# A transformer layer on one core: requests to a two-bank PSUM ring spaced out, and large transfers issued behind the attention loads

## What is computed

```python
# phase 1: conditioned RMS norm, 16 heads of 32, q and k normalised per head
xn = rms_norm(x, g_norm) * (1 + scale) + shift          # scale, shift from cond
q, k, v = heads(xn @ W_qkv); q = rms_norm(q, g_q); k = rms_norm(k, g_k)
o = softmax(q @ k.T * 32 ** -0.5) @ v
x1 = o + o @ W_out
# phase 2: latent attention, rotary parts, causal
kv_d, q_d = n1 @ kv_d_w, n1 @ q_d_w                     # n1 = rmsnorm(x1, ln1_w)
k = concat(kv_d @ k_u_w, rope(n1 @ rope_k_w)); q = concat(q_d @ q_u_w, rope(q_d @ rope_q_w))
h = x1 + softmax(causal(q @ k.T * scale)) @ (kv_d @ v_u_w) @ o_w
# then: shared expert + the two best of seven routed experts, on n2 = rmsnorm(h, ln2_w)
out = x + h + moe(n2)
```

## Time and profile before

| what | value |
|---|---|
| median of three runs | 1292.82 us (1291.26 to 1294.52) |
| the profiled execution, its time | 1290.86 us |
| its span in the trace | 1289.1 us |
| busy: PE, DVE, ACT, POOL | 91%, 58%, 44%, 23% of the span |
| mean granted PE clock | 0.970 of 2.4 GHz |
| transfers | 178.42 MB, 138 GB/s on the mean |

### The profile page before, as it was taken

The page is one execution under the profiler, slowest core; times in us unless marked ns, Lnnn a source line. Parts: engine busy times, 40 slices in busy tenths (PEclk is TensorE's granted clock), DMA queues, the critical chain, the costliest instruction groups (busy, mean ns, idle before and its releaser), DMA issues.

```text
span 1289.1 us, 18670 instructions
## 1 busy us (share of the span) xinstructions
PE 1169.7 (91%) x6059; PEld 825.7 (64%) x6059; DVE 744.4 (58%) x1807; ACT 572.3 (44%) x1248; POOL 290.7 (23%) x244
## 2 busy tenths in 40 slices
PE   5979999999999889999999989989999999999970
PEld 5745555665566446557767757766657888888850
DVE  6565675477545856666565575566364774444433
ACT  3324464345443555455465454455264753222210
POOL 1313122100210031001011200200124464555530
PEclk9979999999999999999999999999899999999995
DMA  7064243125311732352284264265357744555559
GB/s 255 33 180 131 65 136 112 50 86 184 99 50 58 225 107 57 99 189 88 88 259 149 86 234 122 84 201 176 86 186 232 262 152 105 109 108 113 115 134 331
DMA packets 88127, 178.42 MB, mean 138 GB/s; under 512 B 12609, under 2 KB 23265, under 8 KB 86497
## 3 DMA queue, kind: packets, MB, share of 16 engines
q1 hardware_dynamic: 79216, 156.90, 37.4%
q0 software_dynamic: 8512, 19.93, 8.2%
q10 hardware_dynamic: 304, 0.40, 0.2%
HBM read 110.86 MB, written 65.27 MB: 137 GB/s over the span
## 4 chain that ended last, share of the span: by engine, by line
PE 77%; DVE 8%; DMA 5%; ACT 4%; issue 3%; SPq 1%; POOL 0%; DVEq 0%; ACTq 0%; POOLq 0%
PE psum L862 14%; PE psum L681 9%; PE psum L682 8%; PE psum L683 8%; PE psum L846 6%; PE psum L825 6%; PE psum L690 4%; PE psum L940 4%; PE psum L942 4%; PE psum L941 4%; PE psum L967 2%; PE psum L969 2%; PE psum L968 2%; PE psum L909 2%; PE psum L772 2%
## 5 line engine op out<-in xcount | busy, mean ns | idle before, releaser
L1174 ACT ACTIVATE probs<-psum 128x512 f32<-128x512 f32 (+3 forms) x512 | 257.3, 517 | 231.5 <-PE psum L849 120.6
L825 PE MATMUL psum<-stack 96*128 96x512 f32 (+3 forms) x512 | 210.2, 416 | 8.6 <-DMA stack<-split_s 4.0
L1583 DVE TENSOR_REDUCE nmax<-psum 128x1 f32<-128x512 f32 x256 | 170.5, 684 | 77.0 <-PE psum L825 73.2
L846 PE MATMUL psum<-stack 97*128 97x512 f32 (+3 forms) x512 | 197.3, 386 | 16.8 <-ACT probs L1174 15.4
L862 PE MATMUL psum<-probs,vals 128*33 128x512 f32 (+3 forms) x1024 | 209.4, 531 | 0.0
L1586 DVE CUSTOM_DVE_ANT_0 psum<-psum,causal 128x128 f32<-128x128 f32 (+3 forms) x256 | 123.0, 501 | 21.0 <-PE psum L825 19.4
L825 PEld LDWEIGHTS psum<-stack 96*128 96x128 f32 x512 | 100.0, 196 | 46.3 <-issue 23.7
L846 PEld LDWEIGHTS psum<-stack 97*128 97x128 f32 x512 | 99.0, 193 | 40.0 <-ACT probs L1174 25.8
L862 PEld LDWEIGHTS psum<-probs,vals 128*33 128x33 f32 x1024 | 49.8, 112 | 99.6 <-issue 65.5
L681 PE MATMUL psum<-w_hi,xh 128*128 128x512 f32 (+1 forms) x256 | 95.4, 373 | 4.2 <-DVEq L1449 2.5
L682 PE MATMUL psum<-w_hi,xl 128*128 128x512 f32 (+1 forms) x256 | 93.6, 366 | 0.0
(11 more groups left out here) (238 smaller groups left out, 2338.0 us busy)
## 6 DMA issues: line engine op xcount, KB each, us to landing
stack<-split_s SPq DMA_DIRECT2D x378, 128.0 KB, 3.0
split_s<-split SPq DMA_DIRECT2D x64, 512.0 KB, 3.0
xt<-in_x_dram SPq DMA_DIRECT2D x4, 1024.0 KB, 5.2
x_s<-yt SPq DMA_DIRECT2D x4, 1024.0 KB, 5.0
xt<-x_s SPq DMA_DIRECT2D x4, 1024.0 KB, 4.8
yt<-in_x_dram SPq DMA_DIRECT2D x4, 1024.0 KB, 5.6
res<-x_s SPq DMA_DIRECT2D x4, 1024.0 KB, 8.2
acc_s<-yt SPq DMA_DIRECT2D x4, 1024.0 KB, 6.0
```

The source lines that it names most:

```text
L825: sq.filled(nc.tensor.matmul(psum[:, sq.bank(M), 0:n], st[:, 0, t * P:(t + 1) * P], st[:, 1, 0:n], start=True, stop=True), M)
L846: last = nc.tensor.matmul(psum[:, bank, lo:S], st[:, 1, t * P:(t + 1) * P], st[:, 0, lo:S], start=True, stop=not masked)
L1174: sk.cleared(nc.scalar.activation(probs[:, M % NX, lo:S], psum[:, sk.bank(M), lo:S], ACT.Exp, scale=SCALE), M)
L1583: sq.cleared(V.tensor_reduce(out, psum[:, sq.bank(M), :], AX.X, ALU.max, negate=True), M)
```

## The change

Nothing is computed differently, and no instruction comes or goes apart from a few that wait. Numbers in the table of steps change, one line moves the last `x` key of a sequence from step 63 to step 0 of the next block, and SP's large transfers move by three steps, which puts each behind the six loads of its neighbourhood. `w_raw` moves from step 46 to 41.

```diff
-        put((23, 27, 31, 35) if phase(j) == 1 else (25, 29, 33, 37), each("out", i, NT))
+        put((23, 28, 31, 36) if phase(j) == 1 else (25, 29, 33, 39), each("out", i, NT))
         if phase(i) == 2:
-            put((28, 33, 36, 41), each("square2", i, NT))
-            put((43, 43, 44, 44), each("norm2", i, 4))
-            put((47, 47, 49, 49), each("scale2", i, NT))
-            put((51, 52, 54, 55), each("x2", i, NC))
-            put((59, 62), each("router", i, 2))
+            put((28, 33, 36, 42), each("square2", i, NT))
+            put((44, 44, 45, 45), each("norm2", i, 4))
+            put((46, 46, 47, 47), each("scale2", i, NT))
+            put((49, 52, 54, 55), each("x2", i, NC))
+            put((60, 62), each("router", i, 2))
+    if k and j < NB:
+        put((0,), [("x", j, NC - 1)])
...
-        put((26, 30, 33, 39) if k == B - 2 else (39, 47, 55, 59), each("v", j, NT))
+        put((25, 30, 33, 39) if k == B - 2 else (39, 47, 54, 55), each("v", j, NT))
...
-        put((27, 31, 35, 39), each("v", j, NT))
+        put((27, 31, 36, 41), each("v", j, NT))
...
-        put((60, 61, 62, 63), each("x", after, NC))
+        put((60, 62, 63), each("x", after, NC - 1))
...
-                    if i >= B and m == 14:
+                    if i >= B and m == 17:
                         load_residuals(i)
-                    if m == (22 if k == 0 else 6) and k + 2 < NB:
+                    if m == (25 if k == 0 else 9) and k + 2 < NB:
                         load_x(k + 2)
-                    if i >= 0 and phase(i) == 1 and m == 46:
+                    if i >= 0 and phase(i) == 1 and m == 49:
                         store_x1(i)
...
-                    if k == B - 2 and m == 46:
+                    if k == B - 2 and m == 41:
                         ring.wait_full(sp, ("v", B - 1, NT - 1))
...
-                    if k == B and m == 54:
+                    if k == B and m == 57:
                         ring.wait_full(sp, ("out", B - 1, NT - 1))
```

More of the change, by code:

```diff
@@ L579, in _ @@
                             load_pair(k + next_, q)
-                    if i >= B and m == 14:
+                    if i >= B and m == 17:
                         load_residuals(i)
-                    if m == (22 if k == 0 else 6) and k + 2 < NB:
+                    if m == (25 if k == 0 else 9) and k + 2 < NB:
                         load_x(k + 2)
-                    if i >= 0 and phase(i) == 1 and m == 46:
+                    if i >= 0 and phase(i) == 1 and m == 49:
                         store_x1(i)
-                    if i >= 0 and phase(i) == 2 and m == 46:
+                    if i >= 0 and phase(i) == 2 and m == 49:
                         store_acc(i)
-                    if i >= 0 and phase(i) == 2 and m == 54:
+                    if i >= 0 and phase(i) == 2 and m == 57:
                         store_x2(i)
-                    if k == B - 2 and m == 46:
+                    if k == B - 2 and m == 41:
                         ring.wait_full(sp, ("v", B - 1, NT - 1))
@@ L602, in _ @@
                         sp.dma_start(ln2row[:, :], ln2_d.rearrange("(a n) -> a n", a=1).broadcast_to([P, D])).then_inc(o2_ld, 16)
-                    if k == NB - 1 and m == 38:
+                    if k == NB - 1 and m == 41:
                         ring.wait_full(sp, ("v", LAST, NT - 1))
```

## The result

The changed kernel is slower, by 0.7%: 1301.56 us in the median of 20 runs (1294.73 to 1306.52) against 1292.75 us of the kernel before, measured beside it in as many. The ratio is 1.0072, with a 95% interval of 1.0055 to 1.0089, or +9.3 us (7.1 to 11.5). The forecast was 1283.6 us with 1275 to 1293 as its range, so the time lies outside it, on the wrong side.

What follows compares the result with a forecast made beforehand. The PE was taken to set the pace, with some 53 us of holes in the blocks. The terms summed to -9.2 us on the profiled 1290.86, so 1281.7; the median lying 2.0 us higher gave 1283.6, range 1275 to 1293.

Steps and rivals of the forecast that it cites:

- Block 7's residuals: Block 7, step 24: residuals now directly ahead of `max_rows` land about 908.2, `scores_t` waits for them: +0.7 us.
- The low clock stays: Block 7, step 24: the half-speed clock from 906.90 for 6.8 us, behind a 2.27 us hole, remains after the change.
- block 7 would then gain: Rival, chance 0.15: small transfers pass large ones, `wo_raw` is in time, block 7 gains 2.5 us; 1276 us.
- Second norm and router: Blocks 5 and 6: `x2` 0 starts earlier, -2.6 us; block 7: 0; `router` 0 one step later: -1.0 us.
- the second rival: The DVE is the bound that holes hide; 10.3 us of gains come to nothing, 1293.9 us; chance 0.20.
- The circle: Blocks 3 to 6: `turn` 1 k waits through `out` 3, `o_hi`, `o_lo`, +3.4 us; `v` 2 one step later, -2.8.
- The early blocks: `v` 3 earlier -1.6, `out` 3 spaced -1.1, block ends (0 to 3, 5) -2.5, exponential at block start -1.4 us.
- The weights: Block 2: `w_raw` at step 41 removes waits for `max_rows`, -4.6 us; block 4: `wo_raw` and `ln_row` late, +4.3 us.
- the signs: What would show it, among others: block 4 has a hole of 4 to 5 us and a low clock behind it.
- 0.10 for slower: Chance of a slower kernel: backlog behind `out` 3 and `turn_o` 0 costs up to 4.1 us a block, 1296.6 us.
- three terms with a plus: Waits newly made: `turn` 1 k in blocks 3 to 6 +3.4, `ln_row` in block 4 +4.3, `max_rows` in block 7 +0.7 us.

Runs made afterwards that it cites:

- e4: The kernel before with only the load of the residuals moved, from step 14 to 17, behind the stack's loads: 1298.14 us, ratio 1.0048.
- e3: The changed kernel with only the load of the residuals back at step 14: 1294.84 us, ratio 1.0015 to the kernel before.
- e1: The kernel before with all the change's moves of transfers in SP's queue, and the old table of steps: 1297.21 us, ratio 1.0039.
- e5: The kernel before with only `w_raw` moved, from step 46 to 41 of block 2: 1288.35 us, ratio 0.9973.
- e8: The changed kernel with all transfers at their old steps and `out` 3, `v` 2 and `v` 3 of blocks 3 to 6 as before: 1291.13 us, ratio 0.9989.
- e2: The changed kernel with all transfers back at their old steps, so the new table of steps alone: 1294.36 us, ratio 1.0012 to the kernel before.
- e7: The kernel before with the new table's early part; `out`, `v`, second norm, `x2` and router of blocks 3 to 7 as before: 1287.53 us, ratio 0.9969.
- e9: The kernel before with only `wo_raw` and `ln_row` of block 4 moved, from step 54 to 57: 1298.51 us, ratio 1.0043.
- e10: The kernel of e8 with block 7's second norm and router also as before: 1287.84 us, ratio 0.9970 to the kernel before.
- e11: The kernel of e7 with `w_raw` also moved to step 41: 1287.59 us, ratio 0.9966 to the kernel before.
- e6: The kernel before with only block 7's residuals moved, to step 20, one step behind `max_rows`: 1292.24 us, ratio 0.9994.
- e12: The kernel of e11 with block 7's residuals also moved to step 20, one step behind `max_rows`: 1283.33 us, ratio 0.9935 to the kernel before.

## Why the prediction failed

**Block 7's residuals: the step that failed most.** The prediction took the mechanism from `max_rows`'s 6.48 us, and it holds: "if `max_rows` waits for it, `scores_t` of step 24 starts then". The term was mis-sized. It was worked out from one `res` that landed 8.0 us after issue, gave 908.2, and so +0.7 us. Measured are +6.2 us alone (e4) and +7.4 in the changed kernel (e3). Two things were wrong in it.

First, the landing. The last part of `max_rows` came 11.0 us after the issue of `res` in e4, 8.9 in e1 and 12.9 in the changed kernel, not 8.0. The 8.0 us were taken from block 5, where a step is longer and the other transfers stand farther off. For block 7 itself the trace of before had a longer one (transfers issued in 894 to 895):

```profile
res<-x_s SPq DMA_DIRECT2D x1, 1024.0 KB, 10.2
```

Reckoned with 10.2, `max_rows` would have landed at about 910.4; in e4 it was 910.7. Loads that are issued while `res` is under way do not make a long one by themselves: the row of 8.0 us had them too, 4.1 us behind its issue. Over all traces of blocks 5 to 7, `res` took 7.5 to 10.5 us with six loads issued 2.2 to 4.1 us behind it, 7.6 to 10.0 with six loads issued 1 to 2.2 us ahead of it and the next over 7 us behind, and 11.3 to 12.7 with loads 1 us ahead and 4.8 us behind, which only block 7 has in e1, e4 and the changed kernel. In those three all but one to four of the parts land within 8.6 us, and the rest lag by up to 4 us more. Why they lag is open.

Second, the base. "The low clock stays" took the hole of 2.27 us and the low clock of the profiled execution as what the kernel before always pays. Block 7 from step 0 to step 40 in all traces (start to start of `scores_t`):

| residuals at step | kernels | us | low clock in it, us |
|---|---|---|---|
| 14 | before, e3, e5, e8 | 55.0, 53.0, 54.2, 54.3 | 6.8, 3.4, 6.8, 3.4 |
| 14 | e2, e7, e9, e10, e11 | 50.3 to 50.6 | none |
| 17 | e1, e4, changed | 55.2, 58.0, 59.8 | 3.4, 6.8, 10.2 |
| 20 | e6, e12 | 49.8, 50.4 | none |

The profiled base is the longest of nine. In the first row of the table `res` took 8.5 to 10.5 us, in the second 7.5 to 7.9. The means of steps 14 and 17 are 52.0 and 57.7 us, 5.6 apart, which agrees with the medians. From the profiled 55.0 it would have been 2.7.

The rule cited there (the Trainium skill, DMA: Bandwidth & Descriptors, Queues, rings and completion order) has two halves, and the traces agree with both. Of the first, ring order, the changed kernel's `max_rows` is the case: landed at 917.00, just behind `res` at 916.8. Of the second, a small transfer finishing first, e1 is the case: 910.2 against 912.8. What the prediction drew from the second half, that block 7 would then gain, is wrong: the PE waited 4.00 us in e1 all the same.

**Second norm and router: -3.6 reckoned, about +2.6 measured** (e8 against e7, with an uncertainty of some 4). For blocks 5 and 6 I took 1.3 us each, and nothing came. The hole at `x2` 0 is 2.36 us and not shorter, because `scale2` 3 ends at 757.66, which is 83.3 us behind the block's first scores (at 674.4) against 82.9 before (755.02, from 672.1). The prediction says itself that the DVE works without a pause up to there; that the PE comes two steps earlier then buys only a wait. The router's wait fell from 1.07 to 0.66 us in block 5, and the exponential at step 45 came 0.6 us later (e10 against e7), which undid that. In block 7 the term was 0 by the words "less PE work to hide the DVE in"; that ought to have been a plus. It is the second rival (the DVE is the bound), but only for this group.

**The circle: +0.6 reckoned (3.4 - 2.8), 3.0 measured.** Hole at `turn` 1 k: start to start 1.11 to 1.17 us, against 0.85. Gain at `v` 2: 0.4 us of 1.5 each, not 0.7. And `probs` at step 45 is late by 1.34 us in blocks 5 and 6, against 0.55 before. Most of that is the second norm's, as e8 and e10, which have no circle, show with 1.17; 0.17 us in each of blocks 4 to 6, and 0.1 in block 3, are the circle's, the backlog that I had let pass. Together 4 x 0.3 + 4 x 0.3 + 0.6 = 3.0 more than reckoned by the trace, 2.4 by the medians.

**The early blocks: -6.6 reckoned, -4.0 measured (e7).** `v` 3's wait of 1.05 us is gone, and the exponential at the block's start waits 0.44 us in place of 1.1. Wrong was that `x` 3 at step 0 makes no wait: `qk` at step 3 waits 0.63 us for POOL's `xl` in blocks 1 and 2, and keys at steps 60 and 63 show 0.4 to 0.5.

**The weights.** `w_raw`: -4.6 against -3.5 alone, so right by itself. On top of the early table it brought 0.4 (e11 against e7), and why is open. By length of block 2 in the traces, it is worth 4.5 us with the old table (133.0 against 128.5 on the mean) and 2.2 with the new (130.9 against 128.7). `wo_raw`: +4.3 against +5.6, within its bounds. The ACT stood 5.3 us for `ln_row` in e9, where I had reckoned 2.25 and the 5 us from 667 to 672; the hole of the PE came out about as drawn, 4.25 us from start to start against 4.8. The sum had no term for the low clock behind it, which the prediction named only among the signs; in e9's trace it is 6.8 us longer than before, up to 3.4 us of time. That +4.3 came so near is thus in part luck.

**The account.** Against the forecast: residuals 6.7 us worse, second norm 6.2, `w_raw` 4.2, early table 2.6, circle 2.4, `wo_raw` 1.3, together 23.4 of a miss of 18.5 us (-9.2 to +9.3). The parts overshoot by 4.9, which is within what six such differences can tell. Five transfers were moved by no run alone (`load_x`, the three stores and the shared weights). e1 is 3.3 below the sum of its three parts, so they may have brought some; against it stands the wait of 1.4 to 1.7 us for `max_rows` at step 56 of block 4, in the changed kernel and in e1, which the prediction has no term for. This stays open.

The chances leaned on one column: 0.10 for slower, with a single mechanism behind it, while the sum held three terms with a plus, each a wait newly made. Of these only the circle, at its upper bound, would have carried the sum past 1293. `wo_raw` at its bound of 8 gives 1287.3 us, and the residuals, which cost most, had no bounds at all.

## What to carry to other kernels

A small transfer that the PE needs belongs ahead of the large one in the same queue, and where both are due, let the engine with slack wait for the large one: the swap in e6 was worth the 6 to 7 us between it and e4. A duration read from a trace holds with its neighbours in the queue; before it is used at another place, see what is issued just ahead of it and into it there, and take the row nearest to that place (10.2 us here, not 8.0). A hole read from one profile may not be there in most executions: 2.27 us and a low clock in the profile of before, 0.6 us and none in e9, e10 and e11, where nothing at this place was changed. Moving a consumer up when its producer is already at full work takes cover away from the hole, and can cost the clock as well.

## What the runs showed of the hardware

The scatter from run to run goes with the PE's clock. Over the 35 runs of the kernel before beside e1 to e4 (1285.95 to 1300.54 us) the mean granted clock and the time correlate at -0.91, over the runs of each of the other kernels between -0.63 and -0.95. The mean clock is 0.9678 there, 0.9649 over the 20 runs of the changed kernel. If (1 - clock) times the span is taken as the time lost, an estimate, that is 41.6 us and 45.7 us: some 4 of the 9.3 us are clock, the rest holes. That is rather too much, because the low clock costs nothing while the PE idles, as from 912.6 to 917.04. The stretch at 157.8 us, 6.8 us at half clock in block 0, is such scatter: e6, whose block 0 is that of the kernel before, has the same from 157.6, and takes 126.2 us for the block against 123.0 before; and e2, with the changed table, takes 122.8 against 125.6 in the changed kernel. So one profile cannot size an edit of a few microseconds here.

A hole need not be long for the clock to fall. In e8 the two longest waits of the PE in the 9 us ahead of the fall were 0.80 and 2.21 us.

On one queue, the 4 KB of `max_rows`, issued 1.2 us behind the 1 MB of `res`, took 7.7, 9.8 and 11.7 us (e1, e4, changed). With nothing large ahead of it, it took 1.8 us (e6), which is also the median of all transfers of `max_rows` in each trace. It can land before the large one (e1) and is late all the same.
